# One DRAM scratch for the triangle's operands, with the high rows of two operands in one copy over 128 partitions

## The reference, cut to what matters

```python
block = jnp.einsum('bikc,bkjc->bijc', pp, ab1) + jnp.einsum('bikc,bjkc->bijc', ab2, lp) + ab3 * ip
```

## Time and profile before

| | us |
|---|---|
| median of 3 runs | 1457.52 |
| the profiled execution, its own time | 1466.1 |
| its span | 1464.2 |
| TensorE busy | 1358.6 (93%) |
| mean granted TensorE clock | 0.97 of full |

### The profile page before, as it was taken

How to read it: one execution, slowest core, us unless ns; L and a number is a source line. 1 busy time by engine, 2 the same in 40 slices (tenths; PEclk the granted TensorE clock), 3 DMA queues, 4 the chain that set the end, 5 groups by cost and what they waited for, 6 DMA issues and landing times. The chain is left out here.

```text
span 1464.2 us, 32189 instructions
## 1 busy us (share of the span) xinstructions
PE 1358.6 (93%) x9880; PEld 1139.6 (78%) x9880; DVE 1227.2 (84%) x4156; ACT 984.7 (67%) x2293; POOL 1004.4 (69%) x1557
## 2 busy tenths in 40 slices
PE   5999999999999996898789999699999999999993
PEld 2877778877788876787666666599999999999983
DVE  6998989999998974666699999677888888888996
ACT  3888888888888883333367777345776766767763
POOL 3999999999999994444378888334555555555563
PEclk9999999999999998999899999699999999999997
DMA  9899999999999999989689996211222222222222
GB/s 214 215 251 250 256 243 242 261 252 253 257 249 232 257 253 253 294 262 289 159 256 297 298 301 203 94 45 56 73 84 67 82 83 77 73 87 73 73 59 71
DMA packets 358395, 270.63 MB, mean 185 GB/s; under 512 B 60721, under 2 KB 333075, under 8 KB 358227
## 3 DMA queue, kind: packets, MB, share of 16 engines
q1 hardware_dynamic: 356528, 267.90, 69.3%
q10 hardware_dynamic: 1426, 0.46, 0.2%
q0 software_dynamic: 272, 0.21, 0.1%
HBM read 174.17 MB, written 94.37 MB: 183 GB/s over the span
## 5 line engine op out<-in xcount | busy, mean ns | idle before, releaser
L1517 ACT ACTIVATE hT<-psH_d,b 128x512 f32<-128x512 f32 x288 | 197.9, 689 | 158.7 <-PE psH_d L1557 158.7
L654 PE MATMUL psZ_a<-w_all,xT_a 128*128 128x128 f32 x1728 | 230.1, 276 | 0.5 <-DVE high_lp L729 0.4
L654 PE MATMUL psZ_a<-w_all,xT_block 128*128 128x384 f32 x576 | 214.3, 495 | 8.1 <-DVE low_ab L723 5.1
L654 PEld LDWEIGHTS psZ_a<-w_all,xT_a 128*128 128x128 f32 x1728 | 209.8, 192 | 3.3 <-ACT xT_a L562 2.4
L578 ACT ACTIVATE sig_a<-psZ_a 128x256 f32<-128x256 f32 (+1 forms) x360 | 153.7, 427 | 80.6 <-PE psZ_a L654 49.3
L590 POOL TENSOR_SCALAR shared<-shared,coefs_early 128x128 f32<-128x128 f32 x468 | 203.4, 450 | 0.0
L641 PE MATMUL psT_a<-ident,shared 128*128 128x128 f32 x1152 | 186.1, 274 | 3.4 <-issue 2.0
L641 PEld LDWEIGHTS psT_a<-ident,shared 128*128 128x128 f32 x1152 | 141.2, 142 | 54.4 <-issue 27.1
L1584 POOL TENSOR_TENSOR u_d<-u_d,gamma 128x512 f32<-128x512 f32 x72 | 96.0, 1334 | 124.5 <-ACT u_d L1500 109.3
L1211 DVE TENSOR_SCALAR shared<-shared,coef 128x128 f32<-128x128 f32 x288 | 179.0, 681 | 1.6 <-POOL xh_b L1591 1.6
L1591 POOL TENSOR_TENSOR xh_b<-shared,b 128x512 f32<-128x512 f32 x72 | 93.2, 1294 | 105.8 <-DVE ffn_sum L1652 104.6
(11 more groups left out here) (224 smaller groups left out, 3181.7 us busy)
## 6 DMA issues: line engine op xcount, KB each, us to landing
shared<-in_x_dram SPq DMA_DIRECT2D x48, 512.0 KB, 5.7
scratch_xT<-xT_block SPq DMA_DIRECT2D x36, 512.0 KB, 5.2
shared<-scratch_xT SPq DMA_DIRECT2D x36, 512.0 KB, 5.0
scratch_x<-x_c SPq DMA_DIRECT2D x36, 512.0 KB, 4.1
shared<-scratch_x SPq DMA_DIRECT2D x36, 512.0 KB, 3.6
shared<-in_x_dram SPq DMA_DIRECT2D x48, 256.0 KB, 5.1
shared<-L_conv_protein_pair_dram SPq DMA_DIRECT2D x24, 512.0 KB, 7.3
shared<-in_L_conv_l_pair_dram SPq DMA_DIRECT2D x24, 512.0 KB, 9.2
```

Of the source, the lines that this page charges most:

```text
L654: ins = nc.tensor.matmul(out, turned_x(G, i, t0, size)[:, j * P:j * P + P], rhs[i], start=True, stop=True)
L1517: nc.scalar.activation(hT[:, S % 2, f, :], psH[:, f, :], ACT.Gelu, bias=s["b1"][:, f:f + 1]).then_inc(gelued, 1)
```

## The change

The three scratch tensors become one, `scratch_all`, laid out row by row, then by kind (`pp`, `ab1`, `ab2`, `lp`, in this order) and group; a row is 4 x 8 x 1536 floats (196,608 bytes) long. The stores of the projection go to its parts.

`mov_high` is now one copy to 128 partitions: its source walks over two kinds (`pp` and `ab2`), then over 64 rows, then over the run. `ab1_high` is one copy as well, for groups 1 to 7: its source walks over two starts that lie one float apart, then over the same 64 rows, then over the run (in the second half of the partitions, the first float of the run is no longer written, and one float behind the run is; neither is read). The early and late loads of group 0 keep two copies for `ab1_high`, and have the single `mov_high`. `N_LOADS` falls from 9 to 7 a group, and the waits count accordingly (16 copies for group 0, early and late together).

```diff
     lo, hi = CC * a_lo, CC * a_hi
-    view = lambda name, rows, g: d[name][rows, bass.ds(g, 1), lo:hi].rearrange("b o c -> b (o c)")
+    view = lambda kind, rows: d["s_all"][rows, NCG * KINDS_B.index(kind) + g, lo:hi]
     to = lambda rows=slice(0, P), shift=0: bufs[name][rows, lo + shift:hi + shift]
     low, high, first, second = slice(0, P), slice(P, N), slice(0, 64), slice(64, P)
+    if name == "ab1_high" and a_hi - a_lo < N:
+        return [(to(first, SPARE), view("ab1", high)), (to(second, SPARE - 1), view("ab1", high))]
     if name == "ab1_high":
-        return [(to(first, SPARE), view("s_ab", high, g)), (to(second, SPARE - 1), view("s_ab", high, g))]
+
+        one = view("ab1", high)
+        return [(to(shift=SPARE), bass.AP(one.tensor, one.offset, [[1, 2]] + list(one.ap)))]
     if name == "mov_high":
-        return [(to(first), view("s_pp", high, g)), (to(second), view("s_ab", high, g + NCG))]
+        by_kind = d["s_all"][high].rearrange("b (k g) c -> k b g c", g=NCG)
+        return [(to(), by_kind[0:KINDS_B.index("ab2") + 1:KINDS_B.index("ab2"), :, g, lo:hi])]
...
-N_LOADS = 9
+N_LOADS, N_LOADS_FIRST = 7, 2 * 8
...
-    d["s_ab"] = scratch("scratch_ab", (N, 2 * NCG, N * CC))
-    d["s_pp"] = scratch("scratch_pp", (N, NCG, N * CC))
-    d["s_lp"] = scratch("scratch_lp", (N, NCG, N * CC))
+    d["s_all"] = scratch("scratch_all", (N, len(KINDS_B) * NCG, N * CC))
```

More of the change, by code:

```diff
@@ L356, in chain_step @@
     ins.then_inc(stepped, 1)
+KINDS_B = ("pp", "ab1", "ab2", "lp")
 OPERANDS = ("ab1_high", "ab1_low", "pp_low", "ab2_low", "lp_low", "mov_high", "sta_high")
@@ L375, in operand_loads, with loads_up_to @@
     lo, hi = CC * a_lo, CC * a_hi
-    view = lambda name, rows, g: d[name][rows, bass.ds(g, 1), lo:hi].rearrange("b o c -> b (o c)")
+    view = lambda kind, rows: d["s_all"][rows, NCG * KINDS_B.index(kind) + g, lo:hi]
     to = lambda rows=slice(0, P), shift=0: bufs[name][rows, lo + shift:hi + shift]
     low, high, first, second = slice(0, P), slice(P, N), slice(0, 64), slice(64, P)
+    if name == "ab1_high" and a_hi - a_lo < N:
+        return [(to(first, SPARE), view("ab1", high)), (to(second, SPARE - 1), view("ab1", high))]
     if name == "ab1_high":
-        return [(to(first, SPARE), view("s_ab", high, g)), (to(second, SPARE - 1), view("s_ab", high, g))]
+        one = view("ab1", high)
+        return [(to(shift=SPARE), bass.AP(one.tensor, one.offset, [[1, 2]] + list(one.ap)))]
     if name == "mov_high":
-        return [(to(first), view("s_pp", high, g)), (to(second), view("s_ab", high, g + NCG))]
+        by_kind = d["s_all"][high].rearrange("b (k g) c -> k b g c", g=NCG)
+        return [(to(), by_kind[0:KINDS_B.index("ab2") + 1:KINDS_B.index("ab2"), :, g, lo:hi])]
     if name == "sta_high":
-        return [(to(second), view("s_lp", high, g))]
-    return [(to(), view({"ab1_low": "s_ab", "pp_low": "s_pp", "ab2_low": "s_ab", "lp_low": "s_lp"}[name], low,
-                        g + NCG * (name == "ab2_low")))]
-N_LOADS = 9
+        return [(to(second), view("lp", high))]
+    return [(to(), view(name[:-4], low))]
+N_LOADS, N_LOADS_FIRST = 7, 2 * 8
+def loads_up_to(g):
+    return N_LOADS * (g // 2 + g % 2) + N_LOADS_FIRST * (1 - g % 2)
 STA_GROUPS = -(-OPERAND // (PASSES[3][2] * CH))
@@ L469, in store_out @@
                     sp.wait_ge(multiplied, NG_A * n + PASS_END[i])
-                    dst, groups = (d["s_ab"], d["s_pp"], d["s_lp"])[i], (2 * NCG, NCG, NCG)[i]
+                    first, groups = NCG * KINDS_B.index(("ab1", "pp", "lp")[i]), (2 * NCG, NCG, NCG)[i]
+                    dst = d["s_all"][:, first:first + groups, :]
                     sp.dma_start(dst[0:P, :, bass.ds(CC * BLOCK_A * n, CC * BLOCK_A)],
@@ L801, in may_pack @@
             if q == 0:
-                eng.wait_ge(loaded[par], 16 * N_LOADS * (g // 2 + 2 - par))
+                eng.wait_ge(loaded[par], 16 * loads_up_to(g))
             need(eng, summed, 2 * (Q - 1))
@@ L838, in turn @@
                 if q == 0:
-                    pe.wait_ge(loaded[par], 16 * N_LOADS * (g // 2 + 2 - par))
+                    pe.wait_ge(loaded[par], 16 * loads_up_to(g))
                 need(pe, copied, Q - 1)
```

## The result

The changed kernel takes 1657.5 us (median of 4 runs, 1656.3 to 1657.79), the kernel before beside it 1457.13. The ratio is 1.1335 (95% interval 1.1301 to 1.1369): slower by 13%, where 1630 us and the range 1585 to 1670 were forecast.

A forecast was written before the change was run, and what follows sets the result against it. Loading bounds the triangle phase, by about 2 us a group. With merged copies on two engines, seven 42 us steps and group 0 8.4 us later give 1466.1 + 172.4 = 1638.5, less 8.6: 1630 us; range 1585 to 1670.

The forecast's parts named there:

- The bound before: Triangle phase: a group needs 15.8 us of TensorE but takes 18.0, so loading bounds it by about 2 us.
- How many engines share a merged copy: Group loads: two engines, by outermost counts 2 against 128, at 0.84; the other end was all 16, 1.89 us a copy.
- The price of a row on one engine: Merged copies: 26.0 GB/s an engine, 0.236 us per 6144 B row, 15.1 us for 64 rows.
- the sum: Two engines' group load: 30.2 merged, 7.6 low, 1.9 `sta_high`, 39.7 us; steps taken as 42; profiled execution 1638.5 us.
- the meeting of low copies and merged copies in one half: Group loads: slow engines may run at half rate while others write their half, adding up to 4.7 us; middle taken, 42.
- The 8.6 us: Whole kernel: the profiled execution lay 8.6 us above the median, subtracted from 1638.5 to give 1630 us.
- the allowance for the two engines' rate: Group loads: rate may differ from a sixteenth by some per cent of 278 to 311 us, widening 1599-1655 to 1585-1670.
- Group 0: Triangle start: early `mov_high` takes 10.4 us more, 2.0 covered by queue slack; start 8.4 us later, at 574.7.
- Stores: Projection: same runs and outermost counts, only a longer row pitch; priced 0, bounds 6 us either way.
- SP's issue time: SP issues 32 copies fewer, but its time is hidden now, a set being issued within 6 us: 0.
- the last group's low clock: Group 7 takes 19.8 us, TensorE having waited at low clock; same starting level after the change: 0.
- The faster rival: Triangle: all 16 engines share merged copies, a group loads in 13.2 us, TensorE bounds; -20 us, 1437; chance 0.11.

The follow-up runs named there:

- the layout alone: Changed kernel with both merged operands back to two copies each, in the new single scratch with long rows: 1459.83 us, ratio to before 0.9988.

## Why the prediction was right

- **The bound before** (loading by 2 us a group; a copy over 64 partitions costs as much as one over 128): right. When the two pairs of 64-partition copies are merged over all engines, TensorE becomes the bound and steps fall to 16.0 us.
- **How many engines share a merged copy** was the choice that decided, between two ends that no row told apart. Two engines was right: the DMA share is 0.13, the rate 53 GB/s. The rule in the Trainium skill ("DMA: Bandwidth & Descriptors", "Why a DMA increments its semaphore by 16 and not by 1") is borne out by counts of 2 (share 0.13), 4 (share 0.27) and 64 (all sixteen, by steps of 16.0 us).
- **The price of a row on one engine**, 0.236 us and so 15.1 us a copy: right. Without the low copies the mean step is 32.4 us for the sum's 32.1.
- **The term that was mis-sized is the meeting of low copies and merged copies in one half.** It was bounded by 0 and 4.7 us a step and taken as 2.3; it measured 44.9 - 39.7 = 5.2, just beyond the upper bound. Seven times 2.9 us is 20 us, and with 1.7 us more for group 0 this is nearly all of the distance from +172 to +194. Its mechanism was half right: the slow engines do lose time while the others write, but all sixteen are slowed, to 0.39 us a row and for 12.6 us instead of half rate for 9.5, which the half's 208 GB/s does not give by itself.
- **The 8.6 us** taken off for the slow execution profiled before were a second miss. The changed kernel's profiled execution, 1656.3 us, lay 1.2 us under its own median, 17.8 above the sum's 1638.5 (22 from the later starts, less 4.2 behind the triangle); with the 8.6 and the 1.2 that is, to rounding, the distance of 27.5 from 1630 to 1657.5.
- **The range** held partly by luck. The sum's own bounds, 1599 to 1655 with the stores, end under 1657.5. What took it in was the allowance for the two engines' rate, and that rate was not lower but 26.5 GB/s for 26.0.
- **Group 0** was to start 8.4 us later (0 to 10.4): 10.1. The early `mov_high` was the cause, since with it split group 0 starts at 564.90.
- **Stores, SP's issue time, the last group's low clock** at 0: the first is shown by the layout alone (0.9988), the last by group 7's 19.9 us. SP's issue time was wrong in kind: it rose from 5 to 6 us to about 45 a group. It hardly cost anything by itself, as the step without low copies is within 0.3 us of the two engines' rows.
- **The faster rival** was priced well: 20 us less, and 19.7 measured once all engines take part. The kernel with only `mov_high` on all of them kept steps of 17.4 us, by its trace for a reason that the prediction had not listed, the cycle of the two buffer sets.
- **A misreading** without effect: the highest rates in the earlier trace rows are the 297 to 301 GB/s behind the triangle; the triangle has 262 to 294.

## What to carry to other kernels

Before two copies are merged into one with a longer walk, look at the outermost count of both sides and not at the bytes: 2 x 64 rows ran on two engines and 128, or 64 x 2, on sixteen, for the same bytes. Where a source falls into few blocks, lay the scratch out so that the blocks are evenly spaced rows, or put the long dimension first and let the reader of the tile take the other order. And when a queue that was always full gets slack, price the cycle of the buffers next, not the sum of the copies; a copy added where the queue is full is paid in full at least, here with 30 us for 14 of bytes.

## What had not been expected of the hardware

SP is held up while it issues copies for two engines: seven took it 44 to 46 us, against 5 to 6 for nine before. Low copies beside them added 12.5 us a step for 7.6 us of rows, since all sixteen engines then took 0.39 us a row. The extra store copies with runs of 256 bytes, one float off, cost the projection 30 us for 3.5 MB, twice what their bytes take at the queue's mean rate. A transpose that writes every second column 192 floats away in PSUM took 274 ns, like the plain one.
